# Three graph convolutions in one launch: gathers, casts and far sums re-ordered

## What is computed

```python
def conv(h, W, b):
    m = jnp.concatenate([h[dst], h[src], edge_attr], axis=1) @ W + b
    return jax.ops.segment_sum(m, dst, num_segments=n_nodes)
h = jax.nn.relu(conv(x, W1, b1))
h = jax.nn.relu(conv(h, W2, b2))
return conv(h, W3, b3)
...
x = _layernorm(x + _L0_gnn_ref(...), axis=-1)
```

## Time and profile before

| what | value |
|---|---|
| median of 3 runs | 2801.68 us (2799.05 to 2805.03) |
| the profiled execution | 2796.28 us |
| its span, first to last instruction | 2794.5 us |
| mean granted TensorE clock | 0.981 |
| busy PE, DVE, ACT, POOL | 89%, 74%, 78%, 61% of the span |
| HBM traffic over the span | 185 GB/s |

### The profile page before, as it was taken

How to read it: one execution, slowest core, us unless ns; L and a number is a source line. 1 busy time by engine, 2 the same in 40 slices (tenths; PEclk the granted TensorE clock), 3 DMA queues, 4 the chain that set the end, 5 groups by cost and what they waited for, 6 DMA issues and landing times.

```text
span 2794.5 us, 51850 instructions
## 1 busy us (share of the span) xinstructions
PE 2492.9 (89%) x18243; PEld 1820.8 (65%) x18243; DVE 2057.6 (74%) x4510; ACT 2171.0 (78%) x2972; POOL 1706.8 (61%) x1391
## 2 busy tenths in 40 slices
PE   1599999999999999999978888888887888888887
PEld 0155555556555555556657777877776777777777
DVE  7999999999999999999765555555553555555554
ACT  5799899898888988998517777777775777777776
POOL 5354454454453454554357777777766777777776
PEclk9699999999999999999989999999998999999999
DMA  4443533533534434434548777777775777777774
GB/s 94 126 149 113 180 125 113 189 115 122 179 116 137 167 113 153 151 113 174 193 128 270 250 250 248 244 250 252 246 239 183 246 237 246 237 236 242 241 241 127
DMA packets 257344, 519.32 MB, mean 186 GB/s; under 512 B 153954, under 2 KB 189784, under 8 KB 253889
## 3 DMA queue, kind: packets, MB, share of 16 engines
q1 hardware_dynamic: 152596, 299.50, 32.9%
q10 hardware_dynamic: 57404, 146.14, 13.9%
q0 software_dynamic: 47088, 70.34, 10.0%
HBM read 361.98 MB, written 153.81 MB: 185 GB/s over the span
## 4 chain that ended last, share of the span: by engine, by line
PE 49%; POOL 33%; issue 10%; DVE 5%; ACT 3%; DMA 1%; ACTq 0%; SPq 0%; DVEq 0%; POOLq 0%
POOL far_rows L895 32%; PE ps L1633 14%; PE ps L1604 14%; PE ps L1662 8%; PE ps L1648 3%; PE ps L1681 3%; ACT spread L1050 2%; PE ps L1734 2%; PE ps L1696 1%; PE ps L1699 1%; PE ps L1735 1%; DVE is_key L1274 1%; PE ps L1709 1%; ACT blocks L985 1%; PE ps L1720 1%
## 5 line engine op out<-in xcount | busy, mean ns | idle before, releaser
L895 POOL DMA_INDIRECT far_rows<-parts,far_src x1350 | 1652.2, 1224 | 1039.1 <-issue 368.3
L985 ACT ACTIVATE blocks<-ps 128x505 fp8e4<-128x505 f32 x1875 | 1117.8, 758 | 138.5 <-PE ps L1604 135.7
L1050 ACT CAST spread<-blocks 125x1500 fp32r<-125x1500 fp8e4 x637 | 897.6, 1443 | 250.3 <-PE ps L1648 229.0
L1515 DVE CAST spread<-blocks 125x1500 fp32r<-125x1500 fp8e4 x588 | 570.5, 974 | 606.0 <-PE ps L1648 603.0
L1604 PE MATMUL ps<-is_key,is_low 128*128 128x505 bf16 x1875 | 700.4, 384 | 31.4 <-DMA w_own<-in_L_gnn_W 13.9
L1633 PE MATMUL ps<-blocks,parts 125*128 125x375 fp8e4 x2600 | 719.1, 324 | 4.2 <-ACT blocks L985 2.4
L1274 DVE TENSOR_SCALAR is_key<-from_one,parts 128x500 bf16<-128x500 f16 x1875 | 614.9, 359 | 1.6 <-PE ps L1604 0.9
L1648 PE MATMUL ps<-spread,halves_last 125*128 125x376 f32 x2500 | 499.7, 347 | 87.5 <-ACT spread L1050 83.9
L1648 PEld LDWEIGHTS ps<-spread,halves_last 125*128 125x128 f32 x2500 | 422.5, 191 | 137.1 <-ACT spread L1050 128.1
L1633 PEld LDWEIGHTS ps<-blocks,parts 125*128 125x128 bf16 x2600 | 255.1, 99 | 191.7 <-issue 15.0
L1648 PE MATMUL ps<-spread,halves_kept 125*128 125x376 f32 x1440 | 285.7, 344 | 66.2 <-ACT spread L1050 48.1
(11 more groups left out here) (159 smaller groups left out, 1841.9 us busy)
## 6 DMA issues: line engine op xcount, KB each, us to landing
blocks<-counts SPq DMA_DIRECT2D x250, 937.5 KB, 5.0
counts<-blocks ACTq DMA_DIRECT2D x25, 4687.5 KB
far_rows<-parts,far_src POOLq DMA_INDIRECT x1350
far_masks<-far_masks_kept SPq DMA_DIRECT2D x50, 281.2 KB, 2.9
attr_stage<-in_edge_attr SPq DMA_DIRECT2D x125, 88.0 KB
far_masks_kept<-far_masks SPq DMA_DIRECT2D x25, 281.2 KB, 12.4
h_rows<-rows ACTq DMA_DIRECT2D x49, 128.0 KB
own_sb<-attr_sums ACTq DMA_DIRECT2D x49, 95.7 KB
```

The lines of the kernel that those rows point to most:

```text
L895: nc.gpsimd.indirect_dma_start(far_rows[:, g % 2, j, 0:PARTS * D], None, parts_d[layer], bass.IndirectOffsetOnAxis(ap=far_src[:, g % BATCH ...
L985: nc.scalar.activation(blocks[:, b % 2, :, n * W:(n + 1) * W], build[:, c % BUILD, 0:COLS].rearrange("p (t w) -> p t w", w=W), ACT.Copy, s ...
L1050: nc.scalar.copy(spread[0:L, u % SPREAD_RING, :, 0:DENSE], counted(g, t, T)).then_inc(act_spread, 1)
L1515: nc.vector.tensor_copy(spread[0:L, u % SPREAD_RING, :, 0:DENSE], counted(g, t, T)).then_inc(dve_spread, 1)
```

## The change

Five things change. POOL, in `gather_rows` of steps 27 and later where they run beside another step's units: gather j of step g+1 waits for a unit of step g in turn (unit 0, 1, 3, 4, 5, 7, ... 22), not only for the far sum of g-1. ACT: `keep_h` comes behind the cast of unit 6 instead of unit 4, and `give_rows` behind unit 20 instead of 18. DVE at the start of layer 1: after each `halve` it makes the casts of that fifth's odd units, instead of all five halves first. DVE in layer 2: the normalisation is opened at a second place for one more cast, ahead of the wait for the standard deviation. PE in layer 0: the low part of the far rows is multiplied 64 columns wide, alternating between the two halves of the array, without the zero half.

```diff
                 if (g + 1) % BATCHES:
-                    gather_batch(g + 1)
+                    for j in range(FJ):
+                        if j:
+                            pool.wait_ge(spread_used, unit_at(g, j * (FIFTHS * GROUP_OF) // FJ - 1) + 1)
+                        gather_rows(g + 1, j)
...
                 keep_acc(g)
-                spread_act(h, 3, 5)
+                spread_act(h, 3, 7)
                 keep_h(g)
...
                 if h % BATCHES == 0 and h < ALL:
-                    spread_act(h, 5, 7)
                     give_rows(g)
...
                 else:
-                    spread_act(h, 5, 3 * m + 2)
+                    spread_act(h, 7, 3 * m + 2)
                     if g + 2 < ALL:
                         load_attr(act, g + 2)
-                    spread_act(h, 3 * m + 2, 3 * m + 4)
+                    rows_at = 3 * m + 6
+                    spread_act(h, 3 * m + 2, rows_at)
                     give_rows(g)
-                    spread_act(h, 3 * m + 4, FIFTHS * m)
+                    spread_act(h, rows_at, FIFTHS * m)
                     give_nodes(g)
...
                 nc.vector.tensor_reduce(var[:, :], left[:, :, :], axis=X, op=ALU.add).then_inc(var_ready, 1)
+                if amid:
+                    spread_dve(g + 1, amid + 2, amid + 4)
                 dve.wait_ge(std_ready, n + 1)
...
+            first = units_of(BATCHES + 1)
             for q in range(FIFTHS):
                 halve(q)
-            spread_dve(BATCHES + 1, 0, 2)
+                spread_dve(BATCHES + 1, q * first, (q + 1) * first)
...
                 if g % BATCHES == 0:
-                    spread_dve(h, 3, 2 * m + 2)
                     if g == BATCHES:
                         find_bad()
-                    spread_dve(h, 2 * m + 2, FIFTHS * m)
+                    else:
+                        spread_dve(h, 3, FIFTHS * m)
...
                     make_nodes(g, nodes_at)
-                    spread_dve(h, nodes_at + 2, FIFTHS * m)
+                    spread_dve(h, nodes_at + 4, FIFTHS * m)
...
                 for j in range(FJ):
-                    last = nc.tensor.matmul(acc_ps(g, at), far_rows[:, g % 2, j, 2 * D:4 * D],
-                                            far_masks[:, g % 2, j, :], start=False, stop=(j == FJ - 1))
+                    if g < BATCHES:
+                        side = j % 2 * D
+                        last = nc.tensor.matmul(acc_ps(g, at)[side:side + D, :], far_rows[:, g % 2, j, 2 * D:3 * D],
+                                                far_masks[:, g % 2, j, :], start=False, stop=(j >= FJ - 2))
+                    else:
+                        last = nc.tensor.matmul(acc_ps(g, at), far_rows[:, g % 2, j, 2 * D:4 * D],
+                                                far_masks[:, g % 2, j, :], start=False, stop=(j == FJ - 1))
```

More of the change, by code:

```diff
@@ L1692, in sum_far @@
                 pe.wait_ge(far_landed[g % 2], (g // 2 + 1) * FJ * DMA)
-                if g == 0:
+                if g == BATCHES:
                     pe.wait_ge(zeros_ready, 1)
```

## The result

The changed kernel takes 2817.65 us (2812.38 to 2839.29), the kernel before 2800.09 us (2798.90 to 2805.03) on the same chip: a ratio of 1.0058, 95% interval 1.0045 to 1.0071. Slower by 0.6%, where 0.7% faster was forecast. One of the 14 runs of after gave the 2839.29 us, at a mean granted clock of 0.92 (0.963 to 0.971 in the others); without it the highest is 2819.50. The profiled execution of after took 2812.38 us, its span is 2810.6 us, 16.1 us longer than that of before.

What follows compares the result with a forecast made beforehand. POOL and PE were taken to run at one pace in layer 1, POOL setting it after the change. Gains of 6.3 + 1.5 + 1.5 + 0 + 8.4 + 1.0 = 18.7 us took 2801.68 to 2783.0 us; range 2738 to 2812 us.

Steps and rivals of the forecast that it cites:

- The bound: Layers 1 and 2: POOL's gathers are next to set the pace, so only what POOL saves counts.
- PE's 101 us of own savings: Layers 1 and 2: by PE alone, ACT's moved waits would be worth 24 x 1.3 + 24 x 2.9 = 101 us.
- ACT's later waits: Layers 1 and 2: ACT's wait for turned rows goes; PE waits for far rows instead, 1 to 2 us a step.
- POOL's pace in layer 1: Layer 1 gathers: no change from 26.5 us a step, bounds -1.45 and +0.9 us.
- One of the signs named for a wrong forecast: POOL's step in layers 1 and 2: over 0.5 us off 26.5 or 26.6 us would show the forecast wrong.
- Rival 2: Gathers in layers 1 and 2: crowded casts hit more gathers; at +0.04 us a gather 2818 us; chance 0.15.
- POOL's pace in layer 2: Layer 2 gathers: 26.6 us a step, 0.35 us less, 8.4 us gained in all.
- Layer 0: PE's far low matmuls run two at a time, saving 0.25 us a step, 6.3 us; bounds 8 gained, 5 lost.
- The passage into layer 1: Casts behind each fifth's halves: DVE stops for 8.9 us, POOL gains 1.5 us, bounds 0 and 3.
- The unit waits: Gathers released by units in layers 1 and 2: worth 0, since POOL is a whole step behind its release.
- none ended by L1648: Sign in layers 1 and 2: POOL's gaps are all "issue", none ended by PE's units.
- The ends of the layers: Far sum after the last gather: 1.5 us gained at the end of layer 1, 1 us behind layer 2.

Runs made afterwards that it cites:

- the halves alone: The kernel before with only DVE's casts placed behind each fifth's halves at the start of layer 1: 2804.95 us, ratio 1.0005.
- all three pairs of runs: With and without unit waits: the changed kernel 2817.65 and 2815.03 us, with ACT's old order 2795.58 and 2796.78, with casts in two 2684.69 and 2683.23.
- ACT as before: The changed kernel with ACT's waits back in their old order: 2795.58 us, ratio 0.9983.
- the splits: DVE's casts split: on the changed kernel in two 2684.69 us, in four 2716.08; in two on the kernel before with low pairs 2810.44.
- the re-order alone: The kernel before with only ACT's re-ordered waits: 2832.23 us, ratio 1.0121.
- The fill run: The changed kernel with ten unused matmuls of 500 columns on PE ahead of each far sum from step 27 on but 50: 2818.11 us, ratio 1.0072.
- with halves: The changed kernel with each dense DVE cast in two instructions of two tiles: 2684.69 us, ratio 0.9589.
- with quarters: The changed kernel with each dense DVE cast in four instructions of one tile: 2716.08 us, ratio 0.9699.
- low pairs and casts in two: The kernel before with layer 0's far low pairs and each dense DVE cast in two instructions, ACT in its old order: 2810.44 us, ratio 1.0036.

## Why the prediction was wrong

**The bound, right.** Once PE's order is faster, POOL's gathers set the pace, and PE's 101 us of own savings don't come. POOL had a little in hand in layer 1 of before, the lead of 6.3 us, which can be used up once. With the gathers cheaper PE's step is 24.5 us, near the 25 forecast; in after it was 24.4 and 24.3 in the two steps behind the far sum of step 27, while POOL still had a lead from the passage.

**ACT's later waits, right in mechanism.** The wait for turned rows went; PE waits ahead of the far sum in nearly every step, 2.3 us where 1 to 2 was said.

**POOL's pace in layer 1, wrong: this step failed.** "For layer 1 I take no change, since its pattern is now as good as any I see over many steps; bounds -1.45 and +0.9 us a step" measured +1.38, beyond its upper bound. The 25.5 us between steps 28 and 50 are from here; without them the kernel would have been faster. The nearest row that I took, the one step behind a standstill of 7.55 us with gathers of 1.128 us, stood at a low clock (0.84), with PE and so the casts slower than in a running step; it was one row against 22 steps. The crowding was named, in the same paragraph, and priced at nothing. One of the signs named for a wrong forecast came in both layers: the step is 1.33 us off in layer 1 and 0.66 in layer 2, where 0.5 was allowed. The rows for a price were there: a pattern of 26.3 us in which 6.6 of 18 gathers take under 1.0 us and others start together with a cast and pay 0.14 us is an alignment that PE's own cadence gave, and any change of PE's cadence moves it. Rival 2 is the nearest, at 0.15 and at +0.04 us a gather for both layers; it is +0.081 in layer 1 and +0.006 in layer 2. That its 2818 us is the measured time is luck: layer 1 cost twice what it says and layer 2 next to nothing. And the crowded casts don't "hit more gathers": about as many are hit, and each pays more.

**POOL's pace in layer 2, wrong in sign and small.** 26.6 us was forecast, 27.26 measured, 0.27 above before: PE stood here before too, so the crowding was partly there. With the start of the layer it makes +8.0 us for the forecast -8.4.

**Layer 0, right, the term too small.** The forecast's 1.03 - 0.6 - 0.2 is 0.23 us, 5.8 us in all, not 0.25 and 6.3. Before, 18 low matmuls took 1.03 us from start to next; after:

```profile
640.79 1.20 PE L1702 MATMUL ps<-far_masks,far_rows 128*128 128x125 fp8e4 x18
641.92 0.69 PE L1707 MATMUL ps<-far_masks,far_rows 128*64 128x125 fp8e4 x18
642.54 1.03 PE L1610 MATMUL ps<-is_key,is_low 128*128 128x505 bf16 x4
```

From the low sum to the next build 0.62 us instead of 1.03, and 0.09 more ahead of it (641.92 - 640.79 = 1.13, before 1.04): 0.32 us a batch, 8.0 us, the bound of the forecast. If they pair at 57 ns (9 x 57 = 0.51), a change of width costs 0.09 and 0.11 us; the issue at 36 ns each, between which and 57 ns I had split the difference, need play no part. The Trainium skill (TensorEngine Tiling (Array Packing), Key Properties) says that a change of tiling mode drains TensorE. The trace agrees in that each change costs time, 0.09 and 0.11 us; it does not show that a drain is the reason. Of the 10.7 us up to step 25, 2.7 are not accounted for; the halves alone, without pairs, have that gather 4 us later than before, so the start of layer 1 moves by such an amount from run to run.

**The passage into layer 1, right in DVE's course.** The stop of 8.9 us was forecast from rows 8:

```profile
1414.98 0.94 DVE L1520 CAST spread<-blocks 125x1500 fp32r<-125x1500 fp8e4 x1
1424.82 0.94 DVE L1520 CAST spread<-blocks 125x1500 fp32r<-125x1500 fp8e4 x1 [8.90 <-PE ps L1654]
```

POOL gained 5.2 us and not 1.5: the gap of 4.07 us in step 27's gathers went, which I had not looked for. Alone it is worth nothing, by the run of the halves.

**The unit waits, right in price:** nothing, in all three pairs of runs. But the sign "none ended by L1648" did not come (105 of the gaps are put down to the units), and where POOL was ahead, with ACT as before, gathers did wait, up to 4.5 us. **The ends of the layers, about right:** at the end of layer 1 the far sum comes 3.56 us after the last gather's end, not 4.36, a gain of 0.8 for 1.5; behind layer 2 it is 1.5 for 1.0.

```profile
2094.62 1.50 POOL L895 DMA_INDIRECT far_rows<-parts,far_src  x1 [0.30 <-PE ps L1654]
...
2099.68 1.19 PE L1702 MATMUL ps<-far_masks,far_rows 128*128 128x125 fp8e4 x18 [2.16 <-DMA far_rows<-parts,far_src]
```

**What stays open.** That the length of the casts is the price is shown by the splits, and that ACT's re-order brings it by adding and removing that re-order. That it brings it by when casts start against gathers, and not by more meetings, is read from the traces: with ACT as before 13.85 gathers a step meet a cast and take 1.216 us, with the re-order alone 12.9, and they take 1.341. That the crowding behind the standstill is what moves the starts is argued; no run holds PE's mean pace while spreading the casts. The fill run leaves the crowding as it is (8.2 casts a step within 2 us, the longest stretch from one cast to the next 7.4 us) and has the same slow gathers: it fits, but doesn't tell them apart.

## What to carry to other kernels

When a change makes the engines around the bound faster, ask what happens on what the bound shares with them: here PE's gain became denser casts beside POOL's gathers, and a mean of 1.155 us a gather held only for the old cadence. Price the sharing from the rows as a range of alignments, not as the present mean, look at when the two start against each other and not only at how often they meet, and look for the edit that lowers its unit price (shorter instructions on the blocking engine) before the edits that shift the schedule; it also decides whether those are worth anything. And don't take an engine's share of the chain for the bound: here it was 4% and 38% in two kernels with the same time and the same gathers.

## What the runs showed of the hardware

**A gather pays for the piece of DVE's work that it meets, and by when it meets it.** A cast that starts with the gather costs it 0.14 us (1.09 for 0.95); one that started 0.18 us ahead of it, 0.62 us (1.57). With casts of 0.96 us the longest gather behind 1485 us takes 1.82 us in before, 1.90 in after and 2.22 with ACT's re-order alone, with halves 1.32, with quarters 1.15 (0.95 undisturbed). The Trainium skill (SBUF — State Buffer, Who interferes with whom) has the shared port pair held for the whole instruction; the runs agree that the instruction is the unit, since splitting a cast with no gap for anybody between its parts is enough. It costs DVE 0.10 us a cast in two parts and 0.32 in four.

**The granted clock.** Behind a standstill of 2.92 us at the far sum PE ran at the lower of its two levels for a while (18 matmuls 2.05 us for 1.19; after's clock is 0.97 over the span, before's 0.981, the filled one's 0.983), and with another engine as the bound this cost nothing that the fill run could show. Where PE set the pace it did cost: with low pairs and casts in two, a step with a stretch at the lower level took 28.01 us and one without 26.68, although PE stood for no far rows there.
